# A post-norm transformer layer on one core: inverse roots formed on VectorE, the last norm's scaling behind the next norms, the projection's bias added by GpSimd

## What is computed

```
x = layernorm(x + attention(x) @ W_out + b_out)
h = (x - mean) * rsqrt(var + 1e-5) * gamma + beta
y = silu(h @ w1 + fc1_bias)
x = layernorm(x + 0.5 * (y @ w2 + fc2_bias))
```

## Time and profile before

| | |
|---|---|
| Median of 3 runs | 1784.78 us (1783.34 to 1786.6) |
| The profiled execution's own time | 1787.09 us |
| Its span | 1785.2 us |
| TensorE matmuls busy | 1690.5 us, 95% |
| ScalarE busy | 1562.2 us, 88% |
| VectorE busy | 1384.4 us, 78% |
| GpSimd busy | 1352.6 us, 76% |

### The profile page before, as it was taken

The page is one execution under the profiler, slowest core; times in us unless marked ns, Lnnn a source line. Parts: engine busy times, 40 slices in busy tenths (PEclk is TensorE's granted clock), DMA queues, the critical chain, the costliest instruction groups (busy, mean ns, idle before and its releaser), DMA issues.

```text
span 1785.2 us, 53985 instructions
## 1 busy us (share of the span) xinstructions
PE 1690.5 (95%) x21839; PEld 1152.2 (65%) x21839; DVE 1384.4 (78%) x3200; ACT 1562.2 (88%) x3243; POOL 1352.6 (76%) x833
## 2 busy tenths in 40 slices
PE   4799999999999999999999999999999998889986
PEld 2466666666666666666666666666666656666664
DVE  7978798978787878797989897989796845565554
ACT  4599999999999999999998999999999993765676
POOL 3498989898989898989898989888989891222223
PEclk9899999999999999999999999999999999999999
DMA  4003121211111111151212111111111502222300
GB/s 136 13 20 102 22 52 24 51 26 49 25 50 24 50 25 50 26 167 26 49 26 49 26 49 25 49 26 49 26 50 26 172 14 89 71 72 94 120 12 24
DMA packets 113207, 91.82 MB, mean 51 GB/s; under 512 B 73152, under 2 KB 100032, under 8 KB 111808
## 3 DMA queue, kind: packets, MB, share of 16 engines
q1 hardware_dynamic: 112960, 88.38, 18.3%
HBM read 33.82 MB, written 20.97 MB: 31 GB/s over the span
## 4 chain that ended last, share of the span: by engine, by line
PE 65%; ACT 21%; POOL 5%; DVE 4%; issue 4%; DMA 1%; SPq 0%; DVEq 0%; ACTq 0%
PE psum L1010 10%; PE psum L980 10%; PE psum L1014 10%; PE psum L951 7%; PE psum L1127 6%; PE psum L1038 5%; PE psum L1036 5%; PE psum L1040 5%; ACT p_parts L682 5%; ACT p_full L683 5%; PE psum L965 4%; POOL p_parts L578 4%; ACT kb L1214 2%; ACT w_lo L1218 2%; ACT p_full L1218 1%
## 5 line engine op out<-in xcount | busy, mean ns | idle before, releaser
L578 POOL TENSOR_TENSOR p_parts<-p_full,p_parts 128x1024 f16<-128x1024 f32 (+1 forms) x640 | 1161.1, 1841 | 196.4 <-ACT p_full L683 194.4
L682 ACT ACTIVATE p_parts<-psum 128x512 f16<-128x512 f32 (+3 forms) x1280 | 731.0, 571 | 60.6 <-PE psum L1014 35.2
L683 ACT ACTIVATE p_full<-psum 128x512 f32<-128x512 f32 (+3 forms) x1280 | 738.6, 579 | 0.0
L749 DVE TENSOR_REDUCE row_max<-psum 128x1 f32<-128x512 f32 x768 | 484.2, 681 | 16.1 <-PE psum L980 12.7
L1036 PE MATMUL psum<-v,p_parts 128*128 128x65 f16 x4352 | 487.2, 193 | 7.7 <-POOL p_parts L578 4.7
L1038 PE MATMUL psum<-v,p_parts 128*128 128x64 f16 x4352 | 488.7, 194 | 0.0
L1040 PE MATMUL psum<-v,p_parts 128*128 128x65 f16 x4352 | 486.2, 192 | 0.0
L1036 PEld LDWEIGHTS psum<-v,p_parts 128*128 128x128 f16 x4352 | 406.6, 97 | 83.7 <-POOL p_parts L578 12.5
L1010 PE MATMUL psum<-qa,ka 128*128 128x512 f16 (+3 forms) x1280 | 444.0, 348 | 4.0 <-ACT p_full L683 3.5
L1038 PEld LDWEIGHTS psum<-v,p_parts 128*128 128x128 f16 x4352 | 402.7, 97 | 69.6
L1014 PE MATMUL psum<-qb,kb 128*128 128x512 f16 (+3 forms) x1280 | 443.8, 347 | 3.0 <-DVE qb L762 2.9
(11 more groups left out here) (143 smaller groups left out, 2507.2 us busy)
## 6 DMA issues: line engine op xcount, KB each, us to landing
zT_dram<-z_T SPq DMA_DIRECT2D x16, 1024.0 KB, 4.7
qb<-qa SPq DMA_DIRECT2D x128, 64.0 KB, 1.9
ka<-ka SPq DMA_DIRECT2D x128, 64.0 KB, 1.9
shared_z<-zT_dram SPq DMA_DIRECT2D x4, 2048.0 KB, 8.4
x_hi<-zT_dram SPq DMA_DIRECT2D x4, 2048.0 KB, 9.4
shared_z<-xT_dram SPq DMA_DIRECT2D x8, 512.0 KB, 7.5
x_lo<-x_dram SPq DMA_DIRECT2D x8, 512.0 KB, 10.0
out_dram<-qa SPq DMA_DIRECT2D x8, 512.0 KB, 3.3
```

The source lines that it names most:

```text
L578: nc.gpsimd.tensor_tensor(p_lo[:, at % NP, cols], p_full[:, at % NP, cols], p_hi[:, at % NP, cols], ALU.subtract).then_inc(probs_split, 1)
L682: nc.scalar.activation(p_hi[:, at % NP, to], lane_bank(a)[:, P * f:QB], ACT.Exp, scale=1.0 / SCORE)
L683: nc.scalar.activation(p_full[:, at % NP, to], lane_bank(a)[:, P * f:QB], ACT.Exp, scale=1.0 / SCORE).then_inc(lane_read, 1)
L749: nc.vector.reduce_max(most, bank, AX.X).then_inc(ring_read, 1)
```

## The change

Three things change, all in the feed-forward part.

VectorE forms 1/sqrt(var + eps) itself, in `inverse_root`: a first guess from the bits of the number, and two rounds of correction, eight dependent instructions on 128x4. Sqrt, the reciprocal, and all calls of `root` on ScalarE go; ScalarE loads the silu table once, before the blocks.

`normalise` is split into `spread` (statistics and root) and `rescale`. Of the last norm of block i, `spread` stays behind o(i); then `to_norms(i + 2)` comes, and only then the wait for `stored` and the rescale, which raises `res_ready`. `to_norms(1)` moves ahead of step 0. The last norm gets a variance and root buffer of its own.

GpSimd adds the bias of the projection to x in place (`add_bias`), for blocks 0 and 1 ahead of its steps and for block i + 2 behind the subtracts of block i. It waits for x to land, and VectorE waits for `x_biased` in place of x; the instruction for ya goes.

SyncE's and TensorE's code stays as it is.

```diff
@@ -362,8 +362,11 @@
         preload = sb("preload", [P, 1])
-        stats, mv, var_e, std, rstd = (sb(n, d) for n, d in (("stats", [P, TPB, 6]), ("mv", [P, TPB, 2]),
-                                                             ("var_e", [P, TPB]), ("std", [P, TPB]), ("rstd", [P, TPB])))
+        small = w_lo_all[:, 3 * D + 2 * QB:3 * D + 2 * QB + 18 * TPB]
+        stats = small[:, 0:6 * TPB].rearrange("p (t s) -> p t s", t=TPB)
+        mvs = [small[:, (6 + 2 * a) * TPB:(8 + 2 * a) * TPB].rearrange("p (t s) -> p t s", t=TPB) for a in range(2)]
+        var_e, guess, near, part, ratio, bend = [small[:, a * TPB:a * TPB + TPB] for a in range(10, 16)]
+        rstds = [small[:, a * TPB:a * TPB + TPB] for a in range(16, 18)]
         WO, HT, FC, ZO = 0, 2, 4, 6
@@ -394,12 +397,12 @@
         norm_ready, hT_ps, hT_parts, hT_ready = sem("norm_ready"), sem("hT_ps"), sem("hT_parts"), sem("hT_ready")
-        var_ready, std_ready = sem("var_ready"), sem("std_ready")
         fc1_ready, act_ready, a_split = sem("fc1_ready"), sem("act_ready"), sem("a_split")
...
         preloaded = sem("preloaded")
+        x_biased = sem("x_biased")
         silu_done, ffn_consts = sem("silu_done"), sem("ffn_consts")
@@ -408,6 +411,7 @@
         SHIFT_ROWS = 6
+        GUESS_BITS = float(0x5f3759df)
         CONSTS = 13
@@ -1112,10 +1116,21 @@
+            def add_bias(i, k):
+                pool.wait_ge(x_in[k], 16 * ((i - k) // 2 + 1))
+                nc.gpsimd.tensor_tensor(xs[:, k, :, :], xs[:, k, :, :], bo_s.unsqueeze(1).to_broadcast([P, TPB, D]),
+                                        ALU.add).then_inc(x_biased, 1)
             def step(i, k, more):
...
                     nc.gpsimd.tensor_tensor(a_lo[:, f, :], a_scaled[:, f % 2, :], a_hi[:, f, :], ALU.subtract).then_inc(a_split, 1)
+                if more == 2:
+                    add_bias(i + 2, k)
+            pool.wait_ge(biases_in, 16 * 2)
+            add_bias(0, 0)
+            add_bias(1, 1)
             over_blocks(pool, step)
@@ -1197,11 +1212,6 @@
             act.sem_inc(silu_done, START)
-            act.sem_inc(preloaded, START)
-            def root(n):
-                act.wait_ge(var_ready, n + 1)
-                nc.scalar.activation(std[:, :], var_e[:, :], ACT.Sqrt).then_inc(std_ready, 1)
@@ -1217,27 +1227,9 @@
                     last.then_inc(act_ready, 1)
-                    if f == 1 and i and not projects(i - 1):
-                        root(3 * i + 1)
-                    if more and f in ROOTS_AT:
-                        root(3 * i + 2 + ROOTS_AT.index(f))
-                if not more:
-                    root(3 * i + 2)
-                elif projects(i):
-                    root(3 * i + 4)
-                    preload_silu(i + 1)
-            def preload_silu(n):
-                act.wait_ge(preloaded, sum(projects(i) for i in range(n - 1)) + (n > 0) + START)
-                nc.scalar.activation(preload[:, :], b1_s[:, 0:1], ACT.Silu).then_inc(preloaded, 1)
-            ROOTS_AT = (3, 5)
-            root(0)
-            root(1)
-            preload_silu(0)
+            nc.scalar.activation(preload[:, :], b1_s[:, 0:1], ACT.Silu).then_inc(preloaded, 1)
+            act.wait_ge(preloaded, 1)
             over_blocks(act, step)
@@ -1253,22 +1245,44 @@
-            def normalise(chain, src, dst, n):
+            def spread(chain, src, mv, rstd):
...
                 chain.done(last)
-                dve.sem_inc(passed, 1)
                 for t in range(TPB):
...
                 chain.done(last)
-                nc.vector.tensor_scalar(var_e[:, :], mv[:, :, 1], EPS, None, ALU.add).then_inc(var_ready, 1)
-                dve.wait_ge(std_ready, n + 1)
-                chain.done(nc.vector.reciprocal(rstd[:, :], std[:, :]))
+                chain.done(nc.vector.tensor_scalar(var_e[:, :], mv[:, :, 1], EPS, None, ALU.add))
+                inverse_root(chain, var_e, rstd)
+            def inverse_root(chain, of, root):
+                chain.done(nc.vector.tensor_scalar(guess[:, :].bitcast(I32), of[:, :].bitcast(I32), -0.5, GUESS_BITS, ALU.mult, ALU.add))
+                chain.done(nc.vector.tensor_tensor(part[:, :], guess[:, :], of[:, :], ALU.mult))
+                chain.done(nc.vector.tensor_tensor(ratio[:, :], part[:, :], guess[:, :], ALU.mult))
+                chain.done(nc.vector.scalar_tensor_tensor(out=bend[:, :], in0=ratio[:, :], scalar=-10.0 / 3.0, in1=ratio[:, :],
+                                                          op0=ALU.add, op1=ALU.mult))
+                chain.done(nc.vector.scalar_tensor_tensor(out=near[:, :], in0=bend[:, :], scalar=5.0, in1=guess[:, :],
+                                                          op0=ALU.add, op1=ALU.mult))
+                chain.done(nc.vector.tensor_tensor(part[:, :], near[:, :], of[:, :], ALU.mult))
+                chain.done(nc.vector.scalar_tensor_tensor(out=ratio[:, :], in0=part[:, :], scalar=-0.5 * 0.375 ** 3, in1=near[:, :],
+                                                          op0=ALU.mult, op1=ALU.mult))
+                chain.done(nc.vector.scalar_tensor_tensor(out=root[:, :], in0=ratio[:, :], scalar=1.5 * 0.375, in1=near[:, :],
+                                                          op0=ALU.add, op1=ALU.mult))
+            def rescale(src, dst, mv, rstd):
                 for t in range(TPB):
...
                 return last
+            def normalise(chain, src, dst):
+                spread(chain, src, mvs[0], rstds[0])
+                return rescale(src, dst, mvs[0], rstds[0])
@@ -1293,22 +1307,22 @@
-            NORMS, LAST = 9, 3
-            def to_norms(i, k, n):
+            SPREAD = 11
+            NORMS, LAST = 2 * SPREAD + 2, SPREAD
+            def to_norms(i, k):
                 chain = Chain(first_norms, i * NORMS)
                 dve.wait_ge(wo_ready, i + 1)
-                dve.wait_ge(x_in[k], 16 * ((i - k) // 2 + 1) if isinstance(i, int) else (i - k) * 8 + 16)
+                dve.wait_ge(x_biased, i + 1)
                 to = ZO if i == 1 else WO
...
                 dve.wait_ge(wo_read, i + 1 + START)
-                chain.done(nc.vector.tensor_tensor(ya[:, :, :], y[:, :, :], bo_s.unsqueeze(1).to_broadcast([P, TPB, D]), ALU.add))
-                chain.done(normalise(chain, ya, x1, n))
-                last = normalise(chain, x1, xn, n + 1)
+                chain.done(normalise(chain, y, x1))
+                last = normalise(chain, x1, xn)
                 last.then_inc(norm_ready, 1)
@@ -1327,7 +1341,6 @@
                 if more:
-                    to_norms(i + 1, 1 - k, 3 * i + 2)
                     to_hT(i + 1)
@@ -1339,16 +1352,20 @@
-                dve.wait_ge(stored[k], (((i - k) // 2) * 16 if isinstance(i, int) else (i - k) * 8) + START)
-                last = normalise(chain, o, res[:, k, :, :], 3 * i + 4 if more else 3 * i + 2)
+                spread(chain, o, mvs[1], rstds[1])
+                if more == 2:
+                    to_norms(i + 2, k)
+                dve.wait_ge(stored[k], ((i - k) // 2) * 16 + START)
+                last = rescale(o, res[:, k, :, :], mvs[1], rstds[1])
                 last.then_inc(res_ready, 1)
...
             constants()
-            to_norms(0, 0, 0)
+            to_norms(0, 0)
             to_hT(0)
+            to_norms(1, 1)
             over_blocks(dve, step)
```

## The result

The changed kernel takes 1808.45 us (median of 4 runs, 1807.31 to 1814.59) beside 1785.69 us for the kernel before on the same chip: 1.0134 times as long, interval 1.0107 to 1.0161. (Ratios here are those of the means, so this one lies a little above 1.0127, that of the medians.) By the medians it is slower by 22.8 us, where 22.9 were forecast; the interval leaves 19 to 29 us. The profiled execution took 1808.49 us with a span of 1806.7, against 1785.2 before, so 21.5 us are to be found in its timelines.

The account below looks back on a forecast made before the run. TensorE, 95% busy, bounds the kernel; the moved rescale closes a loop through SyncE's store and load. Head +1.2, block 0 -3.8, five periods +29.0, block 6 -2.3, block 7 -2.4, tail +1.2: +22.9, 1807.7 us; range 1783 to 1820.

Parts of the forecast that it names:

- the ring: Feed-forward blocks: out-projection, norms and rescale, store issue, load of z, next out-projection form a closed loop of 42.7 us.
- The undisturbed chain: VectorE from T, a block's first fc1 matmul, to the last rescale's end, nothing held: 14.7 us.
- The held time: VectorE's small instructions wait for GpSimd's subtracts in each block: 5.0 us, last rescale ending at T + 19.7.
- The walk: Step-by-step timing of VectorE against GpSimd's subtracts: first root ends at 7.4, second near 13.8, last rescale at T + 19.7.
- rival (d): Subtracts slip in between rescales on VectorE: 44.8 us per block, +33, 1818 us; chance 0.15.
- The clock: TensorE's idle stretch of 7.5 us before each out-projection halves its clock: 2.4 us, bounds 0 and 3.5.
- Parts 1 and 2: Roots on VectorE, +1.24 us per norm; bias by GpSimd, 2.3 us in idle time, removing ya's 1.22 us from VectorE.
- The four waits: TensorE's waits per block for silu, xn and a_lo twice, 4.1 us in all, go.
- (a): Blocks without GpSimd's holding and the clock loss: 35.3 to 36 us each, 1771.5 us; chance 0.12.
- (b): Only VectorE's roots held and no clock loss: 38.4 us per block, sum +1.4, 1786 us; chance 0.07.
- (c): Clock stays full, or rescales are not held: 40.3 to 40.8 us per block, 1797 us; chance 0.24.
- (e): Load of z isn't held by SyncE's store: 32.8 us per block, some -27, 1758 us; chance 0.02.

Follow-up runs that it names:

- 1: Also `loads_first`: the changed kernel with SyncE's store of a block issued behind the next loads of z and x; 1757.74 us, 0.9848 times before.
- 2: The changed kernel with the last norm's rescale back ahead of the next norms, roots and bias as changed; 1758.42 us, 0.9849 times before.
- 3: The kernel before with only the last norm's rescale moved behind the next norms; 1830.98 us, run again 1832.24 us, 1.0243 times before.
- 4: Also `small_subtract`: the changed kernel with GpSimd's a_lo subtracts covering 8 of 512 columns; 1775.05 us, 0.9944 times before.
- 5: The changed kernel with 64 unused matmuls ahead of each out-projection of block 3 and later; 1800.01 us, 1.0064 times before.
- 6: The changed kernel with ten more dependent 128x4 products on VectorE between the next norms and the last rescale; 1825.19 us, 1.0207 times before.
- loads_first_ya: The changed kernel with loads issued ahead of the store and the bias add (ya) back on VectorE; 1762.64 us, 0.9858 times before.
- before_loads_first: The kernel before with SyncE's loads issued ahead of the store, nothing else; 1787.6 us, 0.9992 times before.

## Why the prediction was right

It named the ring, and the ring decides: cut in the queue (1), cut on VectorE (2), made alone (3), shortened (4, 5) and lengthened (6), each time the result followed, at the furthest with 9 us between expected and measured (4). The agreement of the total is in part luck: 22.9 and 22.8 are nearer to each other than the interval of 19 to 29 us can tell, and in the ring the term that was too small and those that were too large cancel. The sum by its own terms, measured from T to T, in us:

| Term | forecast | measured |
|---|---|---|
| Attention ends | 0 | -0.4 |
| Head, y of block 0 to T(0) | +1.2 | 16.93 - 16.12 = +0.8 |
| Block 0 | -3.8 | 34.22 - 38.54 = -4.3 |
| Five periods | +29.0 | 5 x (42.64 - 36.90) = +28.7 |
| Block 6 | -2.3 | 24.47 - 26.42 = -1.95 |
| Block 7 | -2.4 | 21.54 - 23.91 = -2.4 |
| Tail | +1.2 | 9.74 - 8.76 = +1.0 |
| Sum | +22.9 | +21.5 |

The ring, 42.7 forecast and 42.64 measured, is nearer than its terms, whose errors offset by luck:

| Term of the ring | forecast | measured |
|---|---|---|
| T to the last rescale, undisturbed | 14.7 | 14.1 (0.27 to y, 13.83 from `small_subtract`) |
| VectorE held by GpSimd | 5.0 | 6.2 |
| Store issue to the projection's start | 10.1 | mean 9.8 (9.1 to 10.9) |
| Out-projection at full clock | 10.5 | 10.5 |
| Its loss to the clock | 2.4 | mean 2.1 (1.5 to 2.6) |

**The undisturbed chain** was 0.6 too long. Small instructions follow each other every 0.20 us, not 0.21 (9 of them twice: 0.2), statistics with aggregate take 1.86, not 1.97 (twice: 0.2), and base with its gap 1.13, not 1.25.

**The held time** is the term whose step failed, 5.0 us where 6.2 were measured. The walk put the waits at the roots' instructions, base and the last rescale, and let a subtract wait while the four rescales run. The roots came out close to the walk (1.74 and 0.99 us; forecast 2.0 and, by the end at 13.8, 1.1, though the holds that the walk names for the second root make 1.5). But a subtract doesn't wait while four rescales run: it gets in between two of them, or holds the first. The rescales took 2.22, 2.31 and 3.06 us instead of 1.38, so 0.84, 0.93 and 1.68. Together with the roots' 2.73 that is 6.2. This is rival (d)'s mechanism, which had a chance of 0.15 against the forecast's 0.40; priced there at 7.1, it was there with 6.2, and the ring still didn't come to 44.8 because three other terms were smaller by 0.3 to 0.6 each. The trace agrees with the Trainium skill (SBUF — State Buffer, section "Who interferes with whom") in that the later of two such instructions waits for the whole of the other, 1.04 us where the subtract had 1.03 left; and that the hold ends with each instruction, as the forecast's sentence on it allowed, is what the three rescales show. Which of two is the later one can't be told from the recorded starts: base's, 1553.81, stands 0.16 us behind that of the subtract which it held, and the second rescale's 0.03 us ahead of that of the subtract which held it.

**The clock** did what the head had shown: it fell to half 2.2 to 4.0 us into the five waits (2.4 in the head, where the prediction read 2.7 out of the earlier trace rows), was full again 3.0 to 5.4 us after the matmuls restart, 2.1 us lost where 2.4 had been reckoned from 24 matmuls of another shape. Experiment 5 gives the term by another way: with the wait filled the projection is 2.1 us shorter, and the period 1.8.

**Parts 1 and 2** went as written. The four waits went, block 0 by itself being 4.3 us shorter; with the ring open a block takes 32.68 us (forecast 32.8). The add of the bias takes 2.34 us (forecast 2.3) behind an x that lands at T + 30.7 (forecast 31), and hides.

**The rivals.** (a), a ring of 35.3 to 36 us without disturbance, did not come; `small_subtract` comes to 35.4 us a block, but only with the subtracts nearly removed, and with some of the clock's loss in it. (b) and (c) fall with the held rescales and the clock. (e) priced an open ring at 1758; `loads_first` opens it and measures 1757.74, which shows that the whole distance between the change and a gain is the store in front of the load.

What stays open is a rule for how many holds a train meets. It changes with where the train falls (`loads_first_ya`, where ya moves the trains, has 2.23, 2.22 and 2.21 us where `loads_first` has 2.22, 2.31 and 5.09, the last of them with the add of the bias in it), but no run varied ScalarE's pace, which spaces the subtracts. Why the load of z needs 8.5 us in one block and 10.3 in another, which moves the ring by as much, wasn't tried either.

## What to carry to other kernels

When a step is moved later, ask which queue waits for its signal, and read what is queued behind that waiting entry: here one store that waits in SyncE's queue for a result held a load of 2 MB that didn't depend on it, and made four stages into a ring, so that each microsecond was paid in every block. Put loads ahead of stores whose data come late; that cost nothing where it wasn't needed (`before_loads_first`) and saved 50 us where it was. And price small instructions beside GpSimd by where they fall in its pattern, not by their own 0.16 us.

## What the runs showed of the hardware

- A train of VectorE instructions lets a waiting GpSimd instruction in between two of them: four rescales of 128x256 took 1.38 us alone, 2.22 or 2.31 with one subtract of 128x512, 3.06 with two, and 5.09 with two and an add of 128x1024. The holding goes both ways: a subtract took 2.40 instead of 1.15 us beside base and a rescale.
- Whether TensorE's clock falls in a short wait isn't told by the length of the wait alone: in `small_subtract` it was half after an idle stretch of 2.19 us and full after one of 2.17, and the 96 matmuls behind them took 12.14 and 10.48 us. In the first case it fell when the matmuls had already run for 0.7 us (0.98 in the stretch 1566 to 1567, 0.50 in the next). ya's 1.2 us in the head of `loads_first_ya` cost 2.1 us, since behind its wait of 2.34 us the clock was half for the transposes.
- 64 matmuls of no use in a wait made the kernel 11 us faster, though the projection in block 1 started later, at T + 30.5 instead of T + 29.4 (1.16 us idle before it, full clock).
